# A term of rows without neighbours moves from two VectorE operations per head to sixteen TensorE products per head

## The reference

```python
h = jnp.maximum(_layernorm(x, axis=-1), 0.0)
# layer 0: 8 heads of 32, then one head of 128; layer 2: 4 heads of 32
e = leaky_relu(f1[..., :, None] + f2[..., None, :], 0.2)
e = jnp.where(mask[:, None, :, :], e, NEG)          # NEG = -9e15
att = jax.nn.softmax(e, axis=-1)
hp = jnp.einsum('bhij,bhjd->bhid', att, h)
# layer 1: maximum over the neighbours' rows, two products, layernorm, relu
# layer 3: mean over the incoming neighbours, two products, leaky relu
x = x + ...
```

## Time and profile before

| | |
|---|---|
| median of 3 runs | 8850.98 us |
| profiled execution | 8839.52 us |
| its span | 8837.8 us |
| mean granted TensorE clock | 0.789 of full speed |
| TensorE matmul busy | 5191.4 us (59%) |
| VectorE busy | 5900.0 us (67%) |
| ScalarE busy | 4379.1 us (50%) |
| GpSimd busy | 5258.7 us (60%) |

### The profile page before, as it was taken

The page is one execution under the profiler, slowest core; times in us unless marked ns, Lnnn a source line. Parts: engine busy times, 40 slices in busy tenths (PEclk is TensorE's granted clock), DMA queues, the critical chain, the costliest instruction groups (busy, mean ns, idle before and its releaser), DMA issues. The chain is left out here.

```text
span 8837.8 us, 179248 instructions
## 1 busy us (share of the span) xinstructions
PE 5191.4 (59%) x60584; PEld 4805.7 (54%) x60584; DVE 5900.0 (67%) x7002; ACT 4379.1 (50%) x3594; POOL 5258.7 (60%) x5234
## 2 busy tenths in 40 slices
PE   3673772074775668465775667556865667552036
PEld 3673771063775568464774557554765567551035
DVE  5874881186886778586877778686876677681024
ACT  5643750165745567165735566355725566350034
POOL 0003777576775677576775677276775677576720
PEclk9886886587887788687887889777887888776568
DMA  3114332235232433334323533235333533223210
GB/s 102 40 40 121 66 71 23 53 45 141 62 71 69 109 76 64 77 66 118 66 64 72 123 66 81 58 63 117 62 66 71 124 67 82 63 53 58 25 22 30
DMA packets 307180, 629.05 MB, mean 71 GB/s; under 512 B 113553, under 2 KB 165906, under 8 KB 270610
## 3 DMA queue, kind: packets, MB, share of 16 engines
q0 software_dynamic: 91936, 161.87, 16.9%
q1 hardware_dynamic: 212354, 456.38, 14.7%
q10 hardware_dynamic: 2160, 0.06, 0.0%
HBM read 506.89 MB, written 111.15 MB: 70 GB/s over the span
## 5 line engine op out<-in xcount | busy, mean ns | idle before, releaser
L552 POOL DMA_INDIRECT G<-table,idx x1416 | 1529.0, 1080 | 506.0 <-issue 441.9
L1416 PE MATMUL ps<-Hn,AT 128*128 128x99 bf16 x12288 | 1774.0, 216 | 0.0
L1416 PE MATMUL ps<-X,AT 128*128 128x99 bf16 x12288 | 1742.1, 215 | 45.8 <-issue 45.8
L689 ACT ACTIVATE Hn<-Rb,q 128x2048 int8<-128x2048 f32 x768 | 1484.0, 1988 | 88.2 <-PE ps L1416 85.5
L689 ACT ACTIVATE Pbuf<-Rb,q 128x2048 int8<-128x2048 f32 x768 | 1487.6, 1987 | 14.2 <-PE ps L1416 11.2
L544 POOL DMA_DIRECT2D idx<-lists x433 | 259.2, 599 | 2064.8 <-issue 1554.3
L552 POOL DMA_INDIRECT best<-table,idx x1024 | 1134.6, 1108 | 319.1 <-issue 308.1
L1416 PEld LDWEIGHTS ps<-X,AT 128*128 128x128 fp8e4 x12288 | 1245.6, 101 | 62.1 <-issue 62.1
L1416 PEld LDWEIGHTS ps<-Hn,AT 128*128 128x128 fp8e4 x12288 | 1256.2, 102 | 0.0
L1414 PE MATMUL ps<-X,Hn 128*128 128x198 bf16 x6144 | 943.3, 270 | 491.8 <-DVE Hn L941 281.2
L1414 PE MATMUL ps<-Hn 128*128 128x198 bf16 x6144 | 959.7, 272 | 448.5 <-DVE Zs L961 239.5
(11 more groups left out here) (191 smaller groups left out, 11014.6 us busy)
## 6 DMA issues: line engine op xcount, KB each, us to landing
Rb<-in_adj SPq DMA_DIRECT2D x128, 1024.0 KB, 5.9
Rb<-rrows SPq DMA_DIRECT2D x104, 1024.0 KB, 6.5
bytes_A<-A SPq DMA_DIRECT2D x128, 256.0 KB
bytes_AT<-AT SPq DMA_DIRECT2D x128, 256.0 KB
AT<-bytes_AT SPq DMA_DIRECT2D x128, 256.0 KB, 3.6
AT<-bytes_A SPq DMA_DIRECT2D x128, 256.0 KB, 3.6
G<-table,idx POOLq DMA_INDIRECT x1416
h<-Hn SPq DMA_DIRECT2D x16, 1024.0 KB, 4.2
```

The costliest lines, as they stand in the source:

```text
L552: pool.indirect_dma_start(out=dst[:, k, :], out_offset=None, in_=table, in_offset=bass.IndirectOffsetOnAxis(ap=idx[:, slot, k:k + 1], axis ...
L689: act.activation(marks[(u * T + jb) % RING].bitcast(I8), Rb[:, u, :], ACT.Sign, bias=q[:, jb, hs], scale=-1.0).then_inc(s["sg"], 1)
L1416: ins = pe.matmul(both[:, 0, 0:G], A8[:, jb, at], v[:, 0:G], start=False, stop=jb == T - 1, skip_group_check=True)
```

## The change

Each LA and LC layer's `prepare` now also transposes `lone` (128x16, one where a row has no neighbour) on TensorE into 16x128, and VectorE makes `lone_rows` of it: 16 rows by 2048 columns, minus `lone` of tile t in row t's block t, zero elsewhere. In each head, at `jb` 0, TensorE multiplies for each of the 16 tiles 128 columns of `lone_rows` (16 rows, float32) with 16 rows of `hsum` (33 columns), ahead of the tile's pair, into the first 33 columns of the sums that `finish_head` subtracts. Lines 965 and 967 go. `POST` and `MINNED`, the numbers of chained operations, follow. TensorE's `heads` waits for two more semaphores once per layer.

```diff
@@ prepare, VectorE
                 v.end()
+                if L is not LB:
+
+                    plain(dve)
+                    dve.wait_ge(s["lT"], b + 1)
+                    dve.scalar_tensor_tensor(lone_rows.rearrange("p (t i) -> p t i", t=T),
+                                             ps[0:T, 3, 0:P].rearrange("p (o i) -> p o i", o=1).broadcast_to([T, T, P]), -1.0,
+                                             ident[0:T, 0:T].rearrange("p (t o) -> p t o", o=1).broadcast_to([T, T, P]),
+                                             ALU.mult, ALU.mult).then_inc(s["lr"], 1)
 
@@ finish_head, VectorE
                 v(dve.tensor_tensor(zt, zt, g0, ALU.subtract))
-                v(dve.tensor_tensor(g0, lone[:, :].rearrange("p (t o) -> p t o", o=1).broadcast_to([P, T, C]),
-                                    hs.rearrange("p (o c) -> p o c", o=1).broadcast_to([P, T, C]), ALU.mult))
-                v(dve.tensor_tensor(zt, zt, g0, ALU.add))
                 v(dve.reciprocal(rden[:, :], zt[:, :, D]))
@@ prepare, TensorE
                 pe.matmul(ps[:, 6, 0:L.H * L.C], ones[:, :], hpart[:, 0:L.H * L.C], start=True, stop=True).then_inc(s["hs"], 1)
+                if L is not LB:
+                    of = lone if L is LA or alone else lone_before
+                    pe.transpose(ps[0:T, 3, 0:P], of[:, :], ident[:, :]).then_inc(s["lT"], 1)
@@ head, TensorE
-                        first = jb == 0 and i % 2 == 0
+                        if jb == 0:
+                            pe.matmul(both[:, 0, 0:L.C], lone_rows[:, at], hsum[0:T, bass.ds(h * L.C, L.C)],
+                                      start=i % 2 == 0, stop=False, skip_group_check=True)
                         pe.matmul(both[:, :, 0:G], greater[:, at], v.rearrange("p (g x) -> p g x", g=2),
-                                  start=first, stop=False, skip_group_check=True)
+                                  start=False, stop=False, skip_group_check=True)
@@ heads, TensorE
                 pe.wait_ge(S[L]["v"], (b + 1) * PREP_CHAIN)
+                pe.wait_ge(S[L]["hsc"], b + 1)
+                pe.wait_ge(S[L]["lr"], b + 1)
@@ constants
-        POST = {LA: 11, LB: 9, LC: 9}
-        MINNED = {LA: 9, LB: 6}
+        POST = {LA: 9, LB: 9, LC: 7}
+        MINNED = {LA: 7, LB: 6}
```

More of the change, by code:

```diff
@@ L165, in build @@
         Pflat = Pbuf[:, :, :].rearrange("p u n -> p (u n)")
+        lone_rows = Pbuf[0:T, 1, :]
         rest = Pbuf[:, 0, :].rearrange("p (t f) -> p t f", t=T)
@@ L235, in build @@
             "pe",
+            "lT",
+            "lr",
             "sg",
@@ L945, in mask, with finish_head @@
                             work()
-            def finish_head(L, h, hn, lone):
+            def finish_head(L, h, hn):
                 s, C, D = S[L], L.C, L.D
@@ L955, in finish_head @@
                 Rh = Rc[:, h * T:(h + 1) * T] if isinstance(h, int) else Rc[:, bass.ds(h * T, T)]
-                hs = hsum[:, h * C:(h + 1) * C] if isinstance(h, int) else hsum[:, bass.ds(h * C, C)]
                 acc = ps[:, :, :].rearrange("p b (n x) -> p (b n) x", n=4)[:, :, 0:L.G].rearrange("p n (s c) -> p n c s", s=3)
@@ L1027, in finish, with heads @@
                     beside_it()
-            def heads(L, b, lone, lists=None):
+            def heads(L, b, lists=None):
                 def head(h, pair, u, following, ended):
@@ L1036, in head @@
                     if ended:
-                        beside.append((END_AT, lambda: finish_head(L, h - 1, n - 1, lone)))
+                        beside.append((END_AT, lambda: finish_head(L, h - 1, n - 1)))
                     if lists:
@@ L1053, in heads @@
                 head(L.H - 1, L.H // 2 - 1, 1, False, True)
-                finish_head(L, L.H - 1, b * L.H + L.H - 1, lone)
+                finish_head(L, L.H - 1, b * L.H + L.H - 1)
             def list_tiles(b, tiles, begin):
@@ L1193, in heads_of @@
                     dve.wait_ge(out_done, b * 16)
-                heads(LA, b, lone, (b, *(LIST_ALL if alone else LIST_LA)))
+                heads(LA, b, (b, *(LIST_ALL if alone else LIST_LA)))
             def sage_sums(b, p):
@@ L1247, in middle @@
                 if alone:
-                    heads(LC, b, lone)
+                    heads(LC, b)
                 else:
-                    heads(LC, b, lone_before, (b + 1, *LIST_LC))
+                    heads(LC, b, (b + 1, *LIST_LC))
             def last_layer(b, following, alone):
@@ L1391, in sums, with head @@
                     ins.then_inc(s["pe"], 1)
-            def head(L, hn, u):
+            def head(L, hn, h, u):
                 s, G = S[L], L.G
@@ L1424, in heads @@
                     for u in range(2):
-                        head(L, b * L.H + hh * 2 + u, u)
+                        head(L, b * L.H + hh * 2 + u, hh * 2 + u, u)
             def square(m, b, weights, following=None):
```

## The result

| | before | after |
|---|---|---|
| median (range) of four runs each, on one chip | 8849.53 us (8836.22 to 8855.86) | 9213.12 us (9196.56 to 9224.54) |
| span of the profiled execution | 8837.8 us | 9222.9 us |
| mean granted TensorE clock | 0.789 | 0.762 |

The ratio is 1.0406, with a 95% interval of 1.0386 to 1.0426. Forecast were 8828 us and a range of 8800 to 8880: both are wrong, and so is the sign.

The account below looks back on a forecast made before the run. POOL's gather was taken to bound most passes, so that faster heads show in five places only. These sum to -16.0 us, with POOL's -7 to -23 us: 8816.5 for the profiled execution, 8828 us as median, range 8800 to 8880.

Parts of the forecast that it names:

- the price of the sixteen products: `jb` 0 of each head: two float32 passes of 0.107 us a product, 3.4 us a head; bounds 0.9 and 5.8 us.
- a rival of the clock: Short products keep TensorE at 1.2 GHz one `jb` longer in 16 heads: +30 us, 8858 us; chance 0.10.
- the forecast's middle heads: Heads between first and last: -1.8 us where VectorE ends last, +0.8 on average where TensorE does, bounds -1.7 and +3.2.
- the 3.85 us of the earlier trace: Late code in `jb` 0 of even heads: where TensorE ends last, no later mask waits, so the products add 3.1 us.
- TensorE becomes the bound: Rival: products cost 5.8 us a head, +33 us, 8884 us; sign turns near 0.27 us a product; chance 0.18.
- Removed operations: Two VectorE operations gone from each head's finish: 1.8 us a head, 1.6 in LC(7); chain to mask 3 1.5 to 1.9 shorter.
- the cheap case: Rival: products cost 0.9 us a head, -57 us with POOL's share, 8794 us; chance 0.06.
- The new operation in `prepare`: One VectorE operation of 2048 elements a partition in each of 16 layers, covered by nothing: 2.3 us a layer.
- The meetings: TensorE against the gather's end: 8 us less late at graph 1, 9 at graph 4, still waiting at 0, 2, 5, 6, 7.
- LC(7): Layer after the last gather: TensorE ends its heads last, each pays +3.0 us, +12.0 us together.
- the 1.8 us of the forecast: POOL's gather speeds up as VectorE is less busy: 1.8 us a gather, -7 us over the five that bound a pass.
- POOL gains more: Rival: the removed two-input operations had slowed POOL, 3.8 us a gather, -19 in place of -7, 8816 us; chance 0.12.

Follow-up runs that it names:

- e3: Changed kernel with the sixteen products in two runs of eight, ahead of the pairs of tiles 0 and 8: 8970.10 us, 1.0108 of before.
- e2: Changed kernel with the products' float32 weights padded with zeros from 16 to 128 rows, one memset a layer: 8959.86 us, a single run.
- e4: Changed kernel with bf16 weights, still 16 rows, and sums split in three bf16 parts, one pass of 99 columns: 8928.03 us, 1.0059 of before.
- e6: Changed kernel with bf16 weights padded to 128 rows and sums in three bf16 parts, products still between the pairs: 8799.51 us, 0.9922 of before.
- e8: Changed kernel with bf16 products of 128 rows, sums in three parts, as one run of sixteen behind `jb` 2: 8808.30 us, 0.9940 of before.
- e7: Changed kernel with its float32 products of 16 rows as one run of sixteen behind `jb` 2's pairs: 8888.81 us, 1.0028 of before.
- e5: Changed kernel without the sixteen products, their term left out, a same-sized operation keeping denominators off zero: 8788.65 us, 0.9918 of before.
- e10: Changed kernel with the two removed VectorE operations kept in each head, reading head 0's sums: 9239.88 us, a single run.
- e9: Changed kernel with the products' float32 weights padded with zeros to 64 rows, one memset a layer: 9232.15 us, a single run.

## Why the prediction was wrong

**The step that failed is the price of the sixteen products**, "0.214 us a product, 3.4 us a head", with an upper bound of 5.8 us. Measured: 0.44 us at 2.4 GHz and 0.68 at 1.2, 9.3 us a head for fifteen of the sixteen. Three things make it up.
- *The clock.* The two passes were priced from the earlier trace rows, 0.112 us apart, and that figure holds at 2.4 GHz only; at 1.2 GHz it is 0.21 (e3). `jb` 0 is where the lower level reigns: 1081 of before's 1440 spacings there were already 0.25 us. The prediction saw 0.33 against 0.25 us durations in the earlier trace rows and made a rival of the clock, but there it let the pairs get slower for longer; it didn't price the new products at the lower level. This gives 0.43 in place of 0.214 us, 6.9 us a head.
- *The change between 16 and 128 rows*, 0.23 to 0.28 us a product (after against e2; 0.20 to 0.23 in bf16, e4 against e6). It was in no bound. The upper bound of two loads of 183 ns assumed products of one kind in a row; a product between unlike neighbours can be dearer than that.
- *Together* they keep TensorE in `jb` 0 for 14 us, all of it at the lower level in the windows above, where before had 4.4.

The Trainium skill, "TensorE: Matmul & The Clock Gate", section "LDWEIGHTS (loading the stationary operand)", gives a load about P / 1.2 ns whatever its rows. For runs of like loads the trace agrees at 2.4 GHz (0.11 us, e3) and not at 1.2 GHz (0.21 us); for 16 or 64 rows between loads of 128 it doesn't agree at either. Its section "Weight-path perf modes — Fast Weight Load (FWL) and DoubleRow" says that float32 weights don't get the fast load, others of 128 columns do; e8's 0.044 us a product beside 0.11 us a float32 pass is in line with that.

**Who hides the products.** Of the forecast's middle heads most were to swallow 3.4 us. e7's products stand apart from the changes of rows and cost 4.4 us a head, 0.27 a product, which is where the prediction's own sum turns from faster to slower: by it e7 should take the time of before and lie 57 us above the case of nearly free products. It lies 25 us above before (1.0028) and 100 above e5. The reduction waited for TensorE in 52 of 96 heads instead of e5's 32. So less was hidden than the sum had it, or the products, put behind `jb` 2 and followed by pairs at the lower clock, cost more than their own length; no run tells these apart, and none has products of 0.214 us, so whether the forecast's price would have given a faster kernel stays open.

In heads that TensorE ends last the prediction took the 3.85 us of the earlier trace rows for what even heads have. In before's trace a pause of over 3 us among the pairs that the profile puts down to issue stands in 13 of the 96 heads, 11 of them among the 48 even ones, and in after's in 5. So it is the lesser part of the even heads; what that is worth in the sum wasn't measured. The sum itself is uneven in a small thing: the two first heads of a pass have +1 us in graphs 0 to 1 and no term in graphs 2 to 3 and 3 to 4, which moves the total by 2 us.

**The rival "TensorE becomes the bound" was right in its mechanism**, with its turning point of 0.27 us a product: 0.05 to 0.08 us (e6) give a faster kernel, 0.27 (e7) a slightly slower one, and 0.25 to 0.31 (e4, by the tiles) one 0.6% slower. Its price, 5.8 us a head and 8884 us, was too small, and with it the range.

**Removed operations: right.** VectorE's chain from the first reduction to mask 3 goes from 10.63 to 9.01 us (median over the 80 heads that another follows), 1.6 us, within the 1.5 to 1.9 forecast; in e10 it is 10.50 again. Without products the removal is worth 0.82% of the time, 73 us, where the cheap case had -57.

**The new operation in `prepare`: right**, 2278 ns against 2.3 us.

**The meetings.** Without or with cheap products graph 1's lateness goes from 16.2 to 0.6 or 1.5 us (forecast 8 less; POOL then ends last), graph 4's from 87.1 to 84.1 (forecast 9 less). With the change's products nothing of this could be seen: +87 and +76, and passes that POOL was to bound (graphs 2, 5 and 6) are now 50 to 88 us late, which the prediction had named as a sign that it is wrong.

**LC(7):** forecast +12.0 for the last stretch with 3 us a head, measured +47, of which four heads of 46.6 instead of 35.1 us from first pair to last are 46. The sign was right and the price was not. Without products (e5) the heads take 35.3 us, so it goes with them; that e5's stretch is still 6 us longer than before's shows how much varies outside the heads.

**POOL:** its eight gathers together are 31 us shorter than before's in e5 and 28 in e8, 3.9 and 3.4 us a gather, but 7 us longer in e6, whose `finish_head` is the same as e8's. So neither the 1.8 us of the forecast nor the 3.8 of the rival "POOL gains more" is shown. The 148 us in the changed kernel are no gain, since POOL then waits for the table.

## What to carry to other kernels

Price an added TensorE product in the place where it will stand: at the clock that its neighbours' spacing there shows, and beside what stands before and behind it, since weights of another number of rows cost 0.2 to 0.28 us in and out; padding with zeros to the neighbours' 128 rows costs one memset of 0.9 to 1.8 us a layer here (14.6 us over 16 in e6, 28.2 in e2). A float32 operand that is exact in bf16, or splits into three such parts, turns two slow passes into one. And ask which engine each head ends on at the new price: 1.6 us a head saved on VectorE was worth 0.8% of the time with no products on TensorE, and brought heads no nearer to each other where TensorE carried the dear ones (51.76 against 51.80 us).

## What the runs showed of the hardware

- Changing the number of weight rows between TensorE products costs 0.23 us at 2.4 GHz and 0.28 at 1.2 (float32), 0.20 and 0.23 (bf16), in and out together (after against e2, e4 against e6); 16 and 64 rows cost the same (float32, e9). Inside a run of equal products of 16 rows it isn't paid (0.11 and 0.21 us from record to record, e3).
- A float32 product of 128 weight columns and 33 moving columns is two passes of 0.11 us at 2.4 GHz and 0.21 at 1.2 (e3); a bf16 one of 99 columns and 128 rows adds 0.044 (e8) to 0.05 us (e6) at 2.4 GHz, though it moves three times as many columns.
- The clock can fall within a run of float32 products of 16 rows (e7, granted 1.00, then 0.50, TensorE busy throughout), and it stays at 0.51 through a `jb` 0 of such products between pairs (after, 15.00 of 15 us busy), while in `jb` 0 of e6 it rises among bf16 products of 128 rows in 51 of 96 heads. What in a product brings this about no run here tells apart.
